# Moving the experts' weighted rows from a GpSimd product and sum to one VectorE operation a tile

## The reference

```
x = L0_attn_x                                     # (8, 512, 256)
xn = _layernorm(x, axis=-1)
x = x + _L0_attn_ref(xn, ...) + _L0_ffn_ref(xn, ...)

# attention: 16 heads of 64, rotary q and k
scores = einsum('bhqd,bhkd->bhqk', q, k) * SCALE
kb = -p * log1p(a * dist)                         # per head, by distance
attn = softmax(scores + kb); out = (attn @ v) reshaped @ out_w.T

# experts: 16 of them, each takes at most C = 256 tokens
gate = softmax(xr @ Wg); idx = argmax(gate, axis=1)
gathered = expert_out[idx, min(loc, C - 1)]
combined = gathered * (gates_s * valid)[:, None]
```

## Time and profile before

| | us |
|---|---|
| median of 3 runs (lowest, highest) | 1146.76 (1145.97, 1149.74) |
| the profiled execution | 1150.09 |
| its span in the trace | 1148.4 |
| PE busy in the span | 1064.0 (93%) |
| ACT busy | 1021.2 (89%) |
| DVE busy | 1005.8 (88%) |
| POOL busy | 826.6 (72%) |

### The profile page before, as it was taken

How to read it: one execution, slowest core, us unless ns; L and a number is a source line. 1 busy time by engine, 2 the same in 40 slices (tenths; PEclk the granted TensorE clock), 3 DMA queues, 4 the chain that set the end, 5 groups by cost and what they waited for, 6 DMA issues and landing times.

```text
span 1148.4 us, 35585 instructions
## 1 busy us (share of the span) xinstructions
PE 1064.0 (93%) x14470; PEld 776.9 (68%) x14470; DVE 1005.8 (88%) x2050; ACT 1021.2 (89%) x2013; POOL 826.6 (72%) x483
## 2 busy tenths in 40 slices
PE   3547999999799999999999999999999999999977
PEld 2436988887466676676766666767667676776756
DVE  8788999996688999999989888999999988899976
ACT  3797999984589999999999999999999999999985
POOL 5471010002699999899999899989999999999842
PEclk9667999999999999999999999999999999999999
DMA  8885676751148557766766685585667557855564
GB/s 292 311 264 189 208 265 220 240 202 52 33 82 157 113 95 148 130 99 107 167 98 107 130 153 106 95 155 124 101 119 153 112 103 135 153 94 111 112 112 92
DMA packets 383106, 164.75 MB, mean 143 GB/s; under 512 B 336610, under 2 KB 372463, under 8 KB 382944
## 3 DMA queue, kind: packets, MB, share of 16 engines
q1 hardware_dynamic: 368832, 137.98, 57.2%
q0 software_dynamic: 5440, 16.61, 3.9%
q10 hardware_dynamic: 8672, 7.90, 2.3%
HBM read 58.79 MB, written 21.00 MB: 69 GB/s over the span
## 4 chain that ended last, share of the span: by engine, by line
PE 65%; ACT 9%; DMA 8%; DVE 7%; POOL 6%; issue 4%; SPq 0%; POOLq 0%; ACTq 0%; DVEq 0%
PE ps_o L1607 12%; PE ps_s L1572 11%; PE ps_x L1528 10%; PE ps_t L1585 8%; PE ps_x L1547 6%; PE ps_x L1538 6%; PE psh L941 5%; PE pso L956 5%; DMA pt_dma<-prob_parts 4%; ACT prob L1286 2%; DMA ot<-ctx_parts 2%; DVE wlo L874 2%; POOL prob_parts L1163 2%; POOL parts L1157 1%; DMA xt_dram<-xth 1%
## 5 line engine op out<-in xcount | busy, mean ns | idle before, releaser
L1286 ACT ACTIVATE prob<-prob,neg_max 128x512 f32<-128x512 f32 x512 | 365.2, 715 | 4.7 <-DVE neg_max L1424 2.6
L1424 DVE CUSTOM_DVE_ANT_0 prob<-ps_s,strips,score_scale 128x512 f32<-128x512 f32 x512 | 360.4, 746 | 10.3 <-PE ps_s L1572 5.9
L1163 POOL TENSOR_TENSOR prob_parts<-prob,prob_parts 128x1024 f16<-128x1024 f32 x127 | 272.1, 2143 | 78.4 <-ACT prob_parts L1276 78.1
L1572 PE MATMUL ps_s<-parts 32*128 32x512 f16 x3072 | 191.2, 379 | 1.1 <-DVE parts L1473 1.0
L1430 DVE SCALAR_TENSOR_TENSOR pt_pe<-ps_t,pt_pe 128x1024 f16<-128x1024 f32 x128 | 156.0, 1219 | 36.2 <-ACT pt_pe L1270 36.1
L1585 PEld LDWEIGHTS ps_t<-ident,prob 128*128 128x128 f32 x1024 | 110.7, 142 | 58.2 <-issue 38.6
L1153 POOL TENSOR_TENSOR rot<-prods 128x1024 f32<-128x1024 f32 x61 | 144.3, 2365 | 3.2 <-DVE prods L1390 3.2
L1528 PE MATMUL ps_x<-xcur,wqkv_hi 128*128 128x512 f16 x480 | 143.7, 381 | 2.2 <-DVE pt_dma L1390 1.3
L1585 PE MATMUL ps_t<-ident,prob 128*128 128x128 f32 x1024 | 140.7, 281 | 3.8 <-DVE pt_pe L1430 3.8
L771 POOL DMA_DIRECT2D expert_dram<-xa x16 | 17.9, 1120 | 173.1 <-ACT xa L816 173.1
L1276 ACT CAST prob_parts<-prob 128x1024 f16<-128x1024 f32 x127 | 132.9, 1046 | 4.0
(11 more groups left out here) (219 smaller groups left out, 2599.4 us busy)
## 6 DMA issues: line engine op xcount, KB each, us to landing
raw<-in_L_ffn_w_dram SPq DMA_DIRECT2D x32, 1024.0 KB, 6.2
xa<-in_L_attn_x_dram SPq DMA_DIRECT2D x8, 512.0 KB, 9.1
slots_dram<-zeros POOLq DMA_DIRECT2D x4, 1024.0 KB, 8.9
xt_dram<-xth SPq DMA_DIRECT2D x8, 512.0 KB, 6.5
xa<-slots_dram SPq DMA_DIRECT2D x16, 256.0 KB, 5.3
expert_dram<-xa POOLq DMA_DIRECT2D x16, 256.0 KB, 5.0
xcur<-xt_dram SPq DMA_DIRECT2D x8, 512.0 KB, 4.8
res<-in_L_attn_x_dram ACTq DMA_DIRECT2D x8, 512.0 KB, 4.1
```

What stands on the lines that cost most here:

```text
L1163: nc.gpsimd.tensor_tensor(prob_parts[:, n % 2, 1], prob[:, (2 * n + 1) % 3], prob_parts[:, n % 2, 0], ALU.subtract).then_inc(prob_lo, 1)
L1286: nc.scalar.activation(prob[:, s % 3, q, :], prob[:, s % 3, q, :], ACT.Exp, bias=neg_max[:, 2 * (s % 3) + q:2 * (s % 3) + q + 1], scale=-1 ...
L1424: nc.vector.tensor_tensor_reduce(prob[:, s % 3, q, :], ps_s[u][:], strips[:, HG * j + u, start:start + S], score_scale[:, 0:1], 3.0e38, AL ...
L1572: last = nc.tensor.matmul(ps_s[h][:], parts[rows, 2 * F % 5, a, f, t * P:(t + 1) * P], parts[rows, (2 * F + 1) % 5, c, f, :], start=(i == ...
```

## The change

GpSimd's `combine` goes, with its two operations on 128x512 elements (L1189 and L1191) and the semaphore between them. In its place VectorE has a `combine` that does product and sum in one `scalar_tensor_tensor` for each tile of 128 tokens (128x256 elements), two for each half: `res = got * gate + res`, with `got` and `res` both in SBUF. It stands at the end of quads 10 and 14 (t = 2 of groups 2 and 3), for batch 0 at the end of quads 2 and 6. `source` and `gate_now` get two buffers, so that `load_routes(b)` waits for the combines of batch b - 2 in place of b - 1.

```
-            wait(sp, combined, 2 * b)
-            sp.dma_start(source[:], source_dram[b]).then_inc(routes_loaded, 16)
-            sp.dma_start(gate[:], gate_dram[b]).then_inc(routes_loaded, 16)
+            wait(sp, combined, 2 * b - 2)
+            sp.dma_start(source[:, b % 2], source_dram[b]).then_inc(routes_loaded, 16)
+            sp.dma_start(gate[:, b % 2], gate_dram[b]).then_inc(routes_loaded, 16)
...
-        def combine(b, half):
-
-            pool.wait_ge(gathered[half], 32 * b + 32)
-            pool.wait_ge(residual_loaded, 16 * b + 16)
-            two = slice(2 * half, 2 * half + 2)
-            nc.gpsimd.tensor_tensor(got[:, two, :], got[:, two, :], gate[:, two].unsqueeze(2).to_broadcast([P, 2, M]), ALU.mult).then_inc(weighted, 1)
-            pool.wait_ge(weighted, 2 * b + half + 1)
-            nc.gpsimd.tensor_tensor(res[:, two, :], res[:, two, :], got[:, two, :], ALU.add).then_inc(combined, 1)
...
-                combine(0, 0)
                 low(1, 1)
-                combine(0, 1)
...
-            if b < NB - 1:
-                if j < 2:
-                    gather(b + 1, j)
-                else:
-                    combine(b + 1, j - 2)
+            if b < NB - 1 and j < 2:
+                gather(b + 1, j)
...
+        def combine(b, half):
+
+            dve.wait_ge(routes_loaded, 32 * b + 32)
+            dve.wait_ge(gathered[half], 32 * b + 32)
+            dve.wait_ge(residual_loaded, 16 * b + 16)
+            for i in range(2 * half, 2 * half + 2):
+                last = nc.vector.scalar_tensor_tensor(out=res[:, i, :], in0=got[:, i, :], scalar=gate[:, b % 2, i:i + 1],
+                                                      in1=res[:, i, :], op0=ALU.mult, op1=ALU.add)
+            last.then_inc(combined, 1)
...
+            if n in (2, 6):
+                combine(0, n // 4)
+            if q in (10, 14) and b < NB - 1:
+                combine(b + 1, q // 4 - 2)
```

More of the change, by code:

```diff
@@ L1011, in attention @@
     res = sb("res", [P, TPB, M])
-    source = sb("source", [P, TPB], U32)
-    gate = sb("gate_now", [P, TPB])
+    source = sb("source", [P, 2, TPB], U32)
+    gate = sb("gate_now", [P, 2, TPB])
     prods1 = pt_dma[:].rearrange("p r a q k c -> p (r a q k c)").bitcast(F32).rearrange("p (i s) -> p i s", i=4)
@@ L1032, in attention @@
     gathered = [sem(f"gathered{half}") for half in range(2)]
-    weighted, combined = sem("weighted"), sem("combined")
+    combined = sem("combined")
     scored = sem("scored")
@@ L1180, in gather @@
                     got[:, i, :], None, expert_dram[:, :],
-                    bass.IndirectOffsetOnAxis(ap=source[:, i:i + 1], axis=0),
+                    bass.IndirectOffsetOnAxis(ap=source[:, b % 2, i:i + 1], axis=0),
                     bounds_check=E * C - 1, oob_is_err=False).then_inc(gathered[half], 16)
-        def combine(b, half):
-            pool.wait_ge(gathered[half], 32 * b + 32)
-            pool.wait_ge(residual_loaded, 16 * b + 16)
-            two = slice(2 * half, 2 * half + 2)
-            nc.gpsimd.tensor_tensor(got[:, two, :], got[:, two, :], gate[:, two].unsqueeze(2).to_broadcast([P, 2, M]), ALU.mult).then_inc(weighted, 1)
-            pool.wait_ge(weighted, 2 * b + half + 1)
-            nc.gpsimd.tensor_tensor(res[:, two, :], res[:, two, :], got[:, two, :], ALU.add).then_inc(combined, 1)
         def group(b, j):
```

## The result

| | before | after |
|---|---|---|
| median of the runs, us | 1146.67 (1145.97 to 1149.74, 4 runs) | 1204.65 (1202.95 to 1207.94, 4 runs) |
| profiled execution, us | 1150.1 | 1207.9 |
| its span, us | 1148.4 | 1206.2 |

The ratio is 1.0500, with a 95% interval of 1.0481 to 1.0519: the changed kernel is 5.0% slower. The forecast was 1188.8 us, in a range of 1144.5 to 1213.

The account below looks back on a forecast made before the run. TensorE, busy 100 of 100 us in dense attention, was taken as the bound. The profiled 1150.1 us plus 15 x 2.8 = 42, start - 1.3 + 1.4 = 0, gave 1192.1, or 1188.8 us for the median; range 1144.5 to 1213.

Parts of the forecast that it names:

- two holds without the clock: Dense attention: both operations of a pair held, TensorE waiting 2.8 us at 15 places, clock full; 1188.8 us, chance 0.32.
- its rival with it: Dense attention: two holds, every pause also lowering TensorE's clock, 1.6 us more; 15 x 4.4 us, 1212.8 us, chance 0.12.
- The hold: Dense attention: VectorE's operation with two SBUF inputs waits for GpSimd's running `multiply`, 1.0 us for the first.
- the gather's 1.89 us: Sign from an earlier stage: GpSimd's gather, 1.03 us median, took 1.89 beside a VectorE operation with two SBUF inputs.
- the row of 16 elements at 45.79: Earlier-stage sign for no hold: small VectorE operation took 0.18 us inside a GpSimd one; rival 1145.5 us, chance 0.23.
- Two holds a pair: Dense attention: `low` takes its 2.16 us turn between the pair's operations, so the second waits too; fill 5's read ends about 1006.0.
- One hold a pair: Rival, dense attention: both operations pass together after `multiply`; TensorE waits 0.65 to 1.05 us a pair, 1157 to 1163 us, chance 0.22.
- no turn: Rival, dense attention: VectorE waits until GpSimd pauses, 7.5 us late; TensorE loses over 6 us each, above 1235 us, chance 0.05.
- 15 places: Dense attention: the 2.8 us wait comes 14 times in batches 1 to 7 and once in batch 0's quad 6.
- The wait of 2.8 us: Dense attention: TensorE wants fill 6 at 1003.26 but fill 5's read ends about 1006.0, so it stands still 2.8 us.
- The start: Start of attention, batch 0: 1.3 us gained from GpSimd's relief, about cancelled by a 1.4 us hold in quad 2.
- GpSimd's relief: GpSimd losing its combines: 1.3 us gained at the start of attention, bounds 0 and 2.5; nothing in the dense part.

Follow-up runs that it names:

- The reduction: Changed kernel with each new VectorE operation replaced by a `tensor_reduce` over the same 256 elements of `got`, without weighting or residual: 1168.41 us, 0.9973 of the kernel before.
- the 16 elements: Changed kernel with each new VectorE operation cut to 16 of its 256 elements, both inputs still in SBUF: 1218.45 us, 1.0374 of the kernel before.
- the run with one operation: Changed kernel with only one of the two new operations at each place, every second tile's sum left out: 1181.02 us, 1.0074 of the kernel before.
- the run with `values` ahead: Changed kernel with TensorE doing values(n - 2) before fill 6 in quads 11 and 15 of batches 0 to 6: 1212.25 us, 1.0318 of the kernel before.
- The last two runs: Changed kernel with VectorE's pairs moved into GpSimd's pauses, batch 0's into VectorE's early waits: 1145.06 us; the same with batch 0's behind quads 2 and 6: 1152.10 us.
- the pairs in the pauses: Changed kernel, whole computation, with VectorE's pairs moved into GpSimd's pauses and batch 0's into VectorE's early waits: 1145.06 us, 0.9981 of the kernel before.
- moving only the start: Kernel before with GpSimd's two combines of batch 0 moved ahead of its first `prob_low`, nothing given to VectorE: 1170.99 us, 0.9989 of the kernel before.
- the repeat: The changed kernel itself, unaltered, run again on another chip: 1228.07 us, 1.0444 of the kernel before.

## Why the prediction was right, and where it was off

The measured 1204.65 us is above the 1180 to 1200 that the prediction gave its likeliest case, two holds without the clock, and below the 1212.8 of its rival with it. It lies in the whole range because that range reached to the rival, which had a chance of 0.12. The mechanism of the wait was right; the size came out between the two cases.

1. **The hold, right.** The prediction took the gather's 1.89 us as the sign that the two engines exclude each other in SBUF. The reduction, with one input and never held, and the 16 elements, held just like 256, show that beside GpSimd's two-input `tensor_tensor`, and that the price is time of waiting. The rival that rested on the row of 16 elements at 45.79 falls. Why that one passed stays open: the GpSimd instruction beside it was of another form (`TENSOR_SCALAR`, one tensor input), the same beside which VectorE's `tensor_scalar` of L442 ran in 0.49 us. Every held operation of these runs that was looked at stood beside a GpSimd `TENSOR_TENSOR`.
2. **Two holds a pair, right, from a weak row.** GpSimd's waiting `low` gets in between the two operations. The durations of 1.28 and 2.35 us, and the run with one operation (a wait of 0.24 us a place in place of 2.5), show it. "One hold a pair" and "no turn" fall. But the gather's case, from which the prediction read it, does not show it: VectorE's second operation there (286.40, 1.23 us) took as long as its first (1.21 us) while the gather ran beside it, so VectorE was not held by it. That this step came out is in part luck.
3. **15 places, right**, 14 and batch 0's quad 6.
4. **The wait of 2.8 us was 2.5.** The 15 waits make 37.1 us in place of 42. The second operation did not wait for `low`'s end and then work 0.4 us: it ended 0.28 us after `low`.
5. **The clock, the mis-sized term.** The prediction's sum put nothing on it and kept 1.6 us a place as a rival, on the ground that TensorE would come from unbroken work, unlike in the earlier trace rows. The runs show that this ground does not hold: behind 13 of 15 pauses out of unbroken work the clock was at 0.50, at 1.7 us each, some 22 us together. Between the landmarks TensorE's busy time grew by 21.5 us. Over the whole span it grew by 17.8 us, since it was lower by 3.7 us elsewhere. The sum with it is 1150.1 + 37.1 + 17.8 = 1205.0, against 1207.9 profiled. The rival's size was right and its "every pause" was not. In the run with `values` ahead no pause up to 1.95 us at the altered places brought it.
6. **The start, counted at 0.1 us, cost 1.8.** ScalarE's wait of 2.52 us is gone, and `rotate` comes at 311.57 in place of 315.86. But the pair in quad 2 is held for two turns as well:

```profile
318.29 3.56 DVE L1406 SCALAR_TENSOR_TENSOR res<-got,gate_now,res 128x256 f32<-128x256 f32 x2
```

   The prediction had one hold of 1.4 us there. From the first gather to the first landmark it is 71.7 us (283.06 to 354.75) against 67.4 (284.03 to 351.42): 4.3 us, of which 2.5 are quad 6's pause. About 1.8 us are left for the start. The last two runs split it: with the pairs in the pauses the same stretch takes 66.1 us, so GpSimd's relief gives 1.3, and the pair in quad 2 costs 3.1.
7. **GpSimd's relief, not told apart.** It was put at 1.3 us, the start alone. The reduction shows 3.2 us (1.5 to 4.8), the pairs in the pauses 2.2 (0.8 to 3.6), moving only the start 1.3 (none to 2.8). These intervals overlap, so it is not shown that 1.3 was too low. TensorE's waits for the DMA in the dense part sank from 2.9 to 1.4 us in the changed kernel, which the prediction counted at nothing.
8. **The double buffer**: nothing, right as far as the reduction shows it, which has it and loses nothing.
9. **Three slips in its working.** Not every VectorE operation of the dense part has an input in PSUM: the reciprocal of `read_context` reads `sums`, in SBUF, alone. It is another one-input operation that is never held; all 64 take 195 to 204 ns:

```profile
L1438 DVE RECIPROCAL rsum<-sums x64: 195/203/204, 325.9 to 1140.4; 128x8 f32<-128x8 f32 x64
```

   The DMA issue of 0.72 us was not alone either: VectorE operations on 1 or 2 elements, 0.16 to 0.17 us each, ran beside it. And its chances for the slower cases add up to 0.71 (0.32, 0.12, 0.22 and 0.05), where it says 0.68.

## What to carry to other kernels

Before work goes from GpSimd to VectorE, look at where its inputs lie and what GpSimd does at that moment: beside GpSimd's `tensor_tensor` an operation with both inputs in SBUF waited out the running instruction, whatever its own size, and two in a row waited twice, since the next GpSimd instruction got in between. Its price is the rest of those instructions, not its own 0.47 us, so it belongs where GpSimd pauses, or in a form that was shown not to be held, as `tensor_reduce` was here. Against a TensorE that never waits, count a new pause with what the granted clock may do after it: here a place cost 3.9 us on average, 2.4 of waiting and 1.5 of lower clock, and pauses of 1.0 to 1.95 us cost no clock at 14 of 14 places.

## What the runs showed of the hardware that I had not expected

- A `tensor_scalar` on 128x256 float32 with a single tensor input, in SBUF, was held like one with two beside GpSimd's `tensor_tensor` (844 to 2228 ns); a `tensor_reduce` on the same input was not (407 to 413 ns). Beside GpSimd's `tensor_scalar` a VectorE `tensor_scalar` of that size took 399 to 486 ns.
- GpSimd, whose instructions are long, loses little to VectorE's short ones: 0.17 us (2.31 against 2.14), while VectorE loses up to 2.1 us to it. Behind a long VectorE operation it lost more: 0.86 us for the gather of the earlier trace rows (1.89 against 1.03).
- A held operation shows its waiting as duration: busy time of VectorE rose by 53.6 us, of which 32 x 0.47 = 15 us are work.
- TensorE's granted clock fell to 0.50 behind 13 of 15 pauses of some 2.5 us out of unbroken work, 12 of 15 in the repeat and 7 of 15 at 2.1 us, each time for 1.7 us of full-speed work.
